# Attention values in tiles of 64 keys by 32 columns, one bank of heads for each half of the keys, 8 KB rows in the scratch, and input loads behind the first takes, in a fused decoder layer

## The reference

```python
x = _layernorm(x + _L0_attn_ref(x, ...))          # causal self-attention, 16 heads of 8, scores from a latent of 64
x = _layernorm(x + _L0_xattn_ref(x, ctx, ...))    # 16 heads of 8 over 512 context keys and 256 own keys (causal)
x = _layernorm(x + _L0_ffn_ref(x, ...))           # 128 -> 64, relu 64x16, -> 64, -> 128
# attention:
attn = softmax(q @ k.T * scale)                   # masked with -inf above the diagonal
out  = attn @ v
```

## Time and profile before

| | us |
|---|---|
| median of 3 runs | 290.76 (288.23 to 294.63) |
| the profiled execution | 293.45 |
| its span in the trace | 291.7 |
| PE busy | 241.0 |
| DVE busy | 194.3 |
| ACT busy | 159.8 |
| POOL busy | 99.8 |

### The profile page before, as it was taken

How to read it: one execution, slowest core, us unless ns; L and a number is a source line. 1 busy time by engine, 2 the same in 40 slices (tenths; PEclk the granted TensorE clock), 3 DMA queues, 4 the chain that set the end, 5 groups by cost and what they waited for, 6 DMA issues and landing times.

```text
span 291.7 us, 13772 instructions
## 1 busy us (share of the span) xinstructions
PE 241.0 (83%) x5973; PEld 144.2 (49%) x5973; DVE 194.3 (67%) x429; ACT 159.8 (55%) x367; POOL 99.8 (34%) x250
## 2 busy tenths in 40 slices
PE   8920478689845699999999499999999999999882
PEld 5710336456533446756555156454654465544651
DVE  0830395785232578797999277999889997852652
ACT  1400024455523257676788255988688858879330
POOL 8650074635321142334372101522225212531131
PEclk9985595999977799999999669999999999999998
DMA  4169995101897017353639600000000000000000
GB/s 138 64 202 299 243 205 141 24 8 42 248 186 174 12 57 169 107 117 102 124 106 224 115 3 3 5 5 5 5 3 5 5 5 5 3 5 21 21 18 18
DMA packets 22716, 23.66 MB, mean 81 GB/s; under 512 B 1472, under 2 KB 20224, under 8 KB 22528
## 3 DMA queue, kind: packets, MB, share of 16 engines
q1 hardware_dynamic: 22224, 22.55, 31.7%
q10 hardware_dynamic: 432, 0.23, 0.3%
HBM read 12.62 MB, written 9.96 MB: 77 GB/s over the span
## 4 chain that ended last, share of the span: by engine, by line
PE 42%; DVE 19%; DMA 14%; SPq 9%; issue 7%; ACT 3%; POOL 3%; ACTq 2%; POOLq 0%; DVEq 0%
PE psum L1011 13%; PE psum L1086 10%; DVE pm L869 9%; DMA qk<-shift_rows 6%; DMA qk<-scr_qk 5%; DVE pm L871 4%; PE psum L1106 4%; PE psum L1018 3%; PE psum L958 3%; ACTq L599 2%; ACT probs L774 2%; DMA scr_m<-spl 2%; SPq L635 1%; PE psum L1173 1%; SPq L634 1%
## 5 line engine op out<-in xcount | busy, mean ns | idle before, releaser
L774 ACT ACTIVATE probs<-psum 128x512 f32<-128x512 f32 (+1 forms) x256 | 120.6, 554 | 41.6 <-PE psum L1011 20.9
L1011 PE MATMUL psum<-qk 51*32 51x128 bf16 (+3 forms) x2048 | 63.2, 266 | 31.7 <-DMA qk<-scr_qk 20.9
L871 DVE TENSOR_REDUCE pm<-psum 128x3 f32<-128x384 f32 x128 | 63.5, 550 | 36.6 <-PE psum L1018 36.5
L869 DVE TENSOR_REDUCE pm<-psum 128x1 f32<-128x512 f32 x128 | 79.1, 681 | 7.0 <-PE psum L1011 7.0
L1086 PE MATMUL psum<-probs,v 128*9 128x256 f32 (+1 forms) x1024 | 66.1, 368 | 3.5 <-issue 2.8
L1011 PEld LDWEIGHTS psum<-qk 48*32 48x32 bf16 (+1 forms) x2048 | 35.2, 96 | 56.1 <-DMA qk<-scr_qk 21.5
L1011 PE MATMUL psum<-qk,km 51*32 51x256 bf16 x1024 | 37.9, 278 | 2.8 <-DMA qk<-shift_rows 2.5
L724 POOL TENSOR_SCALAR_AFFINE_SELECT probs<-probs 128x512 f32<-128x512 f32 x32 | 20.3, 640 | 57.0 <-ACT probs L774 56.7
L1086 PEld LDWEIGHTS psum<-probs,v 128*9 128x9 f32 x1024 | 23.2, 91 | 26.0 <-issue 13.8
L1011 PE MATMUL psum<-km,qk 48*32 48x512 bf16 x512 | 35.6, 394 | 0.2
L1018 PE MATMUL psum<-neg,unit_b 64*32 64x256 bf16 x512 | 31.5, 305 | 0.0
(11 more groups left out here) (98 smaller groups left out, 263.7 us busy)
## 6 DMA issues: line engine op xcount, KB each, us to landing
qk<-scr_qk SPq DMA_DIRECT2D x16, 384.0 KB, 6.4
scr_qk<-spl SPq DMA_DIRECT2D x8, 384.0 KB, 5.1
scr_qk<-spl SPq DMA_DIRECT2D x24, 128.0 KB, 5.1
km<-scr_m SPq DMA_DIRECT2D x8, 384.0 KB, 6.8
scr_m<-spl SPq DMA_DIRECT2D x4, 384.0 KB, 3.1
ctxT_sb<-ctxT SPq DMA_DIRECT2D x1, 1024.0 KB, 5.7
scr_m<-spl SPq DMA_DIRECT2D x4, 256.0 KB, 3.5
wb_sb<-wb SPq DMA_DIRECT2D x1, 642.0 KB, 4.5
```

What stands on the lines that cost most here:

```text
L774: nc.scalar.activation(probs[:, ring % PRING, r, 0:cols], bank_of(s)[:, 0:cols], ACT.Exp, scale=SCALE).then_inc(exp_done, 1)
L869: nc.vector.tensor_reduce(pm[:, place, 1 + 4 * qt:2 + 4 * qt], m, axis=AX.X, op=ALU.max).then_inc(reduced, 1)
L871: nc.vector.tensor_reduce(pm[:, place, 2:5], own_blocks(m), axis=AX.X, op=ALU.max).then_inc(reduced, 1)
L1011: last = nc.tensor.matmul(o[STRIP * c:STRIP * (c + 1)], lhs[:, STRIP * c:STRIP * (c + 1)], rhs, start=start, stop=stop, skip_group_check=True)
```

## The change

Eight things change together.

1. **`pv` in halves.** Each `pv` stage becomes two, for keys 0 to 63 and 64 to 127 of the tile, in tiles of 64 rows by 32 columns, the mode of `S` and `T`. Each half adds into a bank of heads of its own, so 6 banks are left for the other stages. The values are stored with zeros beside them, so that three groups of heads lie under one another in a bank and a unit is copied out once (two ACT copies of 128x512) and not after each step.
2. **norm** sums the two halves: 8 matmuls as before, of 108 and 36 columns and not 36.
3. **Scratch.** The features are ordered so that what a partition takes lies together: a take is 48 rows of 8 KB and not 48x8 pieces of 1 KB. A put is issued for each half of the partitions: 8 DMAs for a `qk` and not 4, 6 for an `m` and not 3. For `qk` 0 to 2 SP issues one half and ACT the other.
4. **Loads.** `wb` is issued behind the take of `qk` 1, `x_rows` and the biases behind that of `qk` 2, the context behind that of `qk` 3.
5. **Splits.** The low parts of `qk` 0 to 3 are all DVE's (before only those of `qk` 0). The split buffers are 5 and not 3.
6. **DVE to ACT.** The 12 applies and the copies of the unit matrices move from DVE to ACT. POOL gets two small operations more for each normalisation.
7. **POOL's start.** The masks are half as wide; the value tiles are zeroed (128x2880 and 128x6480 elements) by POOL.
8. **The planner's** costs, ranks and start steps change; all four `qk` of the first phase come early; half the warming matmuls at the start go.

```diff
-FREE_BANKS = 7
-HEADS_BANK = 7
+FREE_BANKS = 6
+HEADS_BANK = 6
-SPL = 3
+SPL = 5
+V2BUFS = 3
-LATE = [(("qk", 0), 0), (("qk", 1), 0), (("v1", 0), 0), (("qk", 2), 0), (("v1", 1), 0),
+LATE = [(("qk", 0), 0), (("qk", 1), 0), (("qk", 2), 1), (("v1", 0), 1), (("qk", 3), 1), (("v1", 1), 3), (("m", 0), 7),
...
-    return s == ("qk", 0)
+    return s[0] == "qk" and s[1] < B
+def on_both_queues(s):
+    return s[0] == "qk" and s[1] < 3
...
-        scr_qk = nc.dram_tensor("scr_qk", [UNITS, P, SLOTS, 2, T], BF16, kind="Internal").ap()
+        scr_qk = nc.dram_tensor("scr_qk", [UNITS, 2, SLOTS, HALF, 2, T], BF16, kind="Internal").ap()
...
+        def put_half(engine, s, r):
+            parts = half(spl[:, i % SPL, :, :], r, HALF)
+                scr = scr_qk[n, r].rearrange("s f a t -> f s a t")
+                engine.dma_start(scr[:, 0:3, :, :], parts).then_inc(put_done[i], 16)
+                engine.dma_start(scr[:, 3:5, 0, :], parts[:, 0:4:2, :]).then_inc(put_done[i], 16)
+                engine.dma_start(scr[:, 3:5, 1, :], parts[:, 3:6:2, :]).then_inc(put_done[i], 16)
+                engine.dma_start(scr[:, 5, :, :], parts[:, 0::5, :]).then_inc(put_done[i], 16)
+        def take_half(engine, s, r):
+                src = scr_qk[n, r].rearrange("s (d p) a t -> (s d) (p a t)", p=PAIRS)
+                engine.dma_start(half(qk[:, n % B], r, DATA).rearrange("k p a t -> k (p a t)"), src).then_inc(qk_in[n], 16)
...
-            nc.gpsimd.memset(v1[:, :, :, HS], 1.0).then_inc(const_v, 1)
-            nc.gpsimd.memset(v2[:, :, :, :, HS], 1.0).then_inc(const_v, 1)
+            nc.gpsimd.memset(v1[:, :, :], 0.0).then_inc(const_v, 1)
+            nc.gpsimd.memset(v2[:, :, :, :], 0.0).then_inc(const_v, 1)
...
-                    nc.scalar.activation(headsT[:, t % (2 * NG), :], heads[:, 0:T], ACT.Copy).then_inc(drained, 1)
+                    for r in range(2):
+                        nc.scalar.activation(headsT[:, t // NG % 2, r].rearrange("p n t -> p (n t)"), heads[r],
+                                             ACT.Copy).then_inc(drained, 1)
...
+                elif what == "apply":
+                    act.wait_ge(rstd_ready, ln_no[s[1:]] + 1)
+                        last = nc.scalar.activation(x1[:, b, i, :], res[:, i, :], ACT.Identity, bias=offset[:, i:i + 1],
+                                                    scale=rstd[:, i:i + 1])
...
-                    if k == 0 and t:
-                        pe.wait_ge(drained, t)
+                    if k == 0 and g == 0 and t:
+                        pe.wait_ge(drained, 2 * (t // NG))
...
-                        last = nc.tensor.matmul(heads[STRIP * j:STRIP * j + HS + 1, q0:T], v, weights, start=(k == 0),
-                                                stop=(k == len(key_tiles(t)) - 1))
-                    last.then_inc(pv_done, 1)
+                        last = nc.tensor.matmul(o, half(v[:, at:end], half_keys, HALF), half(weights, half_keys, HALF),
+                                                start=(k == 0 and g in (0, NG - 1)),
+                                                stop=(k == len(key_tiles(t)) - 1 and g >= NG - 2), skip_group_check=True)
+                    last.then_inc(pv_done[half_keys], 1)
```

More of the change, by code:

```diff
@@ L86 @@
+SP_COST = {"put": 450, "take": 450, "put_lands": 2800, "take_lands": 3000, "context_lands": 3000, "rows": 900,
            "rows_land": 2200}
@@ L172, in run, with issue @@
         return free[engine]
+    def issue(s, r, cost):
+        return max(run("sp", r, cost), run("act", r, cost)) if on_both_queues(s) else run("sp", r, 2 * cost)
     def when(*stages):
@@ L218, in ready @@
                 r = max(r, when(*([("v1", u // 2)] if u < B else [("vm", u - B), ("v2", u - B)])))
-            return max(r, when(("drain", n - 1))) if s[2] == 0 and n else r
+            return max(r, when(("drain", n - 1))) if s[2] == 0 and group(n) == 0 and n else r
         if what in ("ln1", "wo", "mo") and any(x[0] == "apply" for x in chain):
+            return NEVER
+        if what == "mo" and n < B - 1 and ("wo", B - 1) in chain:
             return NEVER
@@ L310, in emit @@
             done[s] = run("act", r + 60, ACT_COST["drain"]) + 60
-            if group(n) == NG - 1:
-                chain.append(("norm", unit(n)))
+            chain.append(("norm", unit(n)))
         elif what == "rows":
@@ L396, in schedule @@
         waiting = [s for s in chain if s[0] not in MISC and ready(s) < NEVER]
+        assert best or waiting, "the order of the stages has no way on"
         if best:
@@ L509, in decoder_layer @@
         t_no = numbered(s for s in plan if s[0] == "T")
-        pv_no = numbered(s for s in plan if s[0] == "pv")
+        half_no = {s: n for what in ("S", "T", "pv") for r in range(2)
+                   for s, n in numbered(s for s in plan if s[0] == what and half_of(s) == r).items()}
         tile_no = numbered(s[1:3] for s in plan if s[0] == "T" and s[3] == 0)
@@ L548, in put_size @@
         def put_size(i):
[L550 removed]
+            return 16 * 2 * puts(splits[i])
         def bank_of(s):
@@ L789, in _ @@
                     nc.scalar.activation(parts_of(s)[0], m, ACT.Copy).then_inc(split_high, 1)
+                elif what == "apply":
+                    kind_, b = s[1], s[2]
+                    act.wait_ge(rstd_ready, ln_no[s[1:]] + 1)
+                    for i in range(QT):
+                        last = nc.scalar.activation(x1[:, b, i, :], res[:, i, :], ACT.Identity, bias=offset[:, i:i + 1],
+                                                    scale=rstd[:, i:i + 1])
+                    last.then_inc({"ln1": x1_ready, "wo": x2_ready, "mo": x3_ready}[kind_], 1)
+                elif what == "put" and on_both_queues(s[1:]):
+                    put_half(act, s[1:], 1)
+                elif what == "take" and on_both_queues(s[1:]):
+                    take_half(act, s[1:], 1)
                 elif what == "rows" and rows_on_act(s[1]):
```

290 lines of the change are left out of this document (167 added, 123 removed).

## The result

The changed kernel takes 334.2 us (median of 4 runs, 333.92 to 337.14) where the kernel before took 290.85 beside it: a ratio of 1.155, 95% interval 1.144 to 1.166. The forecast was 257. Executions of one kernel differ by some per cent with the state they fall in: medians in this text are over all executions, ratios over the faster state alone.

A forecast was written before the change was run, and what follows sets the result against it. It took the first third to wait on DMA and the rest to be DVE's. From 293.45 us, -6.3 -17.3 -12.2 +1.7 gave 259.3, x 0.991 = 257 us; own range 245 to 266, whole range 238 to 279.

The forecast's parts named there:

- Start: Up to the first scores: fewer warming matmuls, casts moved, two queues, later loads; first take landed at 27 us, -6.3 us.
- First phase: From first scores to the first 512-column reduce: 56 us for 73.3, ending at 83 us, about -17 us.
- 12 x 2.07 + 4: DVE's maxima of 12 steps plus low parts of `qk` 2 and 3: 29 us until unit 0's norm at 56.
- 8 issues on SP (4 in all by my estimate): Issuing `qk` 4's put in halves at the hand-off: 8 DMAs, 0.34 us and more each, 4 us in all.
- Second phase: From the first 512-column reduce to the last: 111.6 reduces + 11 other DVE work + 13 = 135.6 us, -12 us.
- The term of 13 for waits: Time without DVE work between first and last 512-column reduce: 12 us kept from before plus 1 for the lost bank.
- `pv` in halves: Value matmuls on PE: two halves side by side cost the same 0.44 us as a full stage; no gain.
- the loads alone (2.9): Trace check on PE: 32 matmuls with 32 loads of 91 ns took 1.76 us, less than the loads' 2.9.
- Tail: Behind the last reduce, 39.05 us before: longer drains and a POOL step in the last two normalisations, +2 us.
- Hand-off late: Rival, 0.13: three `m`'s puts and takes before `qk` 4's take delay the first large reduce 12 us, to 95; 269 us.
- banks bind: Rival, 0.12: six banks for scores and exponentials keep the stretch of large reduces at 147.8 us, 12 more; 269 us.
- Halves in turn: Rival, 0.04: the two value halves run one after the other on PE, 0.88 us a stage; 284 us.

The follow-up runs named there:

- the other order: Order the earlier planner makes for six banks: kernel before with it 309.62 us; changed kernel's halves with it, hand-off and loads of before, 326.01 us.
- the run at 314.07: Changed kernel with full-height values, one heads bank, seven other banks, and the hand-off of before (whole puts, 1 KB rows): 314.07 us, ratio 1.093.
- the kernel with the ranks of before: Changed kernel with the planner's look-ahead thresholds, window and ranks of the kernel before; stage costs, hand-off and halves as changed: 339.07 us, ratio 1.168.

## Why the prediction was wrong

Its sum was 259.3 in the profiled execution's terms; that execution took 333.92 (span 331.9), 75 us more. By its own steps:

**Start: right in its mechanism, 3.5 us short.** The cast was held (3.31 us, above), the first put left at 16.37 (forecast 16.8), the first score matmul came at 29.68 (27): eight half puts took 6.3 us of SP and not 4, and the take was issued at 22.75.

**First phase: 56 us forecast, 86 measured.** Two terms failed. "12 x 2.07 + 4" took DVE's pace for a phase in which DVE was not the bound: the kernel before needed 35.1 us from its first reduce to unit 0's norm, which its own timeline showed (34.1 to 69.2), and the change took 46.8 (30.5 to 77.35; 39.2 with loads and hand-off of before). And "8 issues on SP (4 in all by my estimate)" halved the bytes and kept the price of one DMA: they took 6.5 us, and 18 half puts of three `m` stood before them. In order of time, of the 33.5 us by which the first 512-column reduce came late (116.5 for 83), 21.4 lay before unit 0's norm (77.4 for 56), 6.4 from there to the put of `qk` 4 (18.9 for 12.5), which waited behind those half puts, and 5.9 from the put on (20.3 for 14.4).

**Second phase: 135.6 forecast, 164.2 measured.** The reduces and DVE's other work came out as summed (113.9 + 10.95 for 111.6 + 11). The term of 13 for waits failed: they are 39.3. I carried the waits of one order into another, and 33.8 of the 39.3 us in the new one are waits for PE. The steps that held in the forecast, 7.0 us with no gap, are 7.5 in the best stretch of the changed kernel (260.38 to 267.92).

**`pv` in halves: right as priced, wrong in what it left out.** A pair costs about what a full stage does. I did not see that with twice the matmuls of values come stalls that no wait explains. The prediction's comparison with "the loads alone (2.9)" is no proof, as it adds up loads that lie over one another. The window of that block of full-height values shows it better (length, busy us of PE and PEld, clock, DMA share, GB/s):

```profile
251.26:253.02 1.76, 1.75 (x32) 0.67 (x32) 1.00 0.00 0
```

All 32 loads are busy for 0.67 us together, inside 1.75 us of matmuls. The Trainium skill's rule of "TensorE: Matmul & The Clock Gate", Part 3, by which the prediction took full-height loads for exposed, is not borne out here: they lie beside matmuls, and full height was as fast in the changed kernel (334.34) and faster in the other order.

**The rule on half puts.** The Trainium skill's warning in "DMA: Bandwidth & Descriptors", Rules for kernel authors, against transfers to partition halves was weighed and set aside; its advice was right, 319.72 for 290.27. What the runs show to be paid is the issue on SP and what stands behind it: moving the shift rows to another queue gave 15 of the 29 back. That the halves land sooner, which the page of the changed kernel suggests (2.8 us for 5.1), is not shown: by the medians of the pages, whole puts landed in 2.4 to 5.1 us in the kernels that have them, halves in 2.7 to 3.7.

**Tail: +2 forecast, +14 measured.** The prediction itself says that three steps of exponentials stand in it; I moved it by 2 us, having read the order and priced nothing. In the run at 314.07 all of the 20 us left stood in this place.

**The rivals.** 'Hand-off late' was the nearest (95 us for the first large reduce; it was 116.5) and 'banks bind' is a real 15 us together with its order, by the ratios 22. 'Halves in turn' was false. None of mine held what the runs put in their place: the order that the planner wrote, 23 of the 43 us when it was undone last, with loads and buffers.

How the 43 us divide can't be given as a sum. In the changed kernel, undone one upon another: hand-off 12, full height with seven banks 8, loads and order 23. Put one by one into the kernel before: hand-off 29, the order and banks for six 15 to 22. They do not add. The likely reason is that each moves what PE, which takes its stages in a fixed order, waits for next: moving the shift rows took away a wait of 2.83 us, and a stall of 1.22 became 4.79. Open is what each number of the planner does, since only the whole order was exchanged, and how much of the loss is the lower clock.

## What to carry to other kernels

Where engines run a written order, price the new order as a change of its own: count what stands behind the last piece of the bounding engine's work, in the order and against the old one. On the issuing engine the price went by the DMA here and not by the byte (3 KB took SP 0.79 us, a take of 384 KB 0.30), and a 3 KB transfer that a step waits for doesn't belong behind puts and takes on the same queue. For a phase in which no engine is full, start from its measured length, not from an engine's pace.

## What the runs showed of the hardware

- Puts of 64 partitions took SP 0.61 us each (the median of 88 in the kernel with half puts), puts of 128 partitions 0.49 (of 44 in the kernel before). With twice as many of them the kernel was slower by 29 us.
- Rows of 8 KB were not clearly faster to take than eight pieces of 1 KB: 6.8 for 6.4 us for `qk`, 5.7 for 6.8 for `m`, and no difference in the time of a kernel.
- PE stood still with nothing to wait for 8.6 us in 4 in the kernel before, 26.4 us in 21 in the changed one; 16.7 to 36.3 us in all seven kernels with halves (some 7,000 matmuls), 2.9 to 10.8 in the thirteen without (6,000). The page counts 55 or 56 packets of instruction for the first kind and 46 to 48 for the second. Two of the long ones (4.46 us at 214, 4.79 at 168) begin where takes are landing, though in the first the DMA share is 0.00 for the last 2.4 us. The longest of all, 12.3 us in the kernel with the ranks of before, ends at the first scores against the context, 4.6 us after the take of their keys was issued, and may be a wait that the profile doesn't show. What causes the others stays open.
- A cast of DVE beside a memset of POOL took 3.31 us, 0.43 without. It ended with the memset (15.55 and 15.27 us). An operation of DVE that reads PSUM (`left`, 0.69 us at 11.51) ran beside the same memset unhindered. Moving the memset, together with a free queue for the first take, brought the first reduce from 34.1 to 22.8 us.
